# Gated attention with experts on one core: score products in two halves of 64 rows, value sums over 32 columns

## The chip, the core and the metric

The kernel runs on one core of a Trainium2 chip. The core has engines with a queue of their own each: TensorE (matmuls into PSUM; "PE", its weight loads "PEld"), VectorE ("DVE"), ScalarE ("ACT"), GpSimd ("POOL"), and SyncE ("SP"), which here issues all DMAs. They meet only through semaphores. The metric is device time in microseconds (us), lower is better.

## What is computed

Sixteen batches of 256 rows of width 128 pass through two layers. Each layer has a cross attention over 1601 context rows with 16 heads of 8 columns, a gated residual, then a second block with a gate: in layer 0 eight experts with two picked per row, in layer 1 a self attention plus eight experts. The second cross attention keeps only the 32 greatest scores of each row:

```
# layer 0 cross attention
scores = jnp.einsum('bhqd,bhkd->bhqk', q, k) / jnp.sqrt(jnp.float32(D_K))
attn = jax.nn.softmax(scores, axis=-1)
ctx = jnp.einsum('bhqk,bhkd->bhqd', attn, v)
# layer 1 cross attention
top_scores, top_idx = jax.lax.top_k(scores, 32)
w = jax.nn.softmax(top_scores, axis=-1)
out = jnp.einsum('bhqk,bhqkd->bhqd', w, top_v)
```

## The kernel before, in words

Heads are worked in groups of four (`HG`), four groups to a batch, 64 groups in all. A float32 score is computed as a bf16 product: q and k are split in three bf16 parts each, and six combinations of parts, of 8 columns each, are stacked as 48 rows (`ROWS`). Three further rows carry the row's shift (its maximum, or the least kept score), so that the attention's score product has 51 rows (`ROWX`) and comes out shifted. The tiles `q`, `k_scan`, `k_att` have 128 partitions, and the rows above 51 are filled with zeros once at the start by GpSimd, so every product contracts 128 rows.

For each group of layer 0, a scan finds the maximum of each row: `n0` (L611) multiplies 128 query rows with 512, 512, 512 and 65 keys, one product per step, into two PSUM banks `score` in turn; `n0_max` (L1056, VectorE) reduces each. `row_turn`, `row_minus`, `shift`, `rows_out`, `rows_in` then bring minus the maximum into the stack's three rows through DRAM. After that, for each of 13 chunks of 128 keys, `s_0` (L652) makes the four heads' scores, four products of 256 columns, in one of two `wide` PSUM tiles (two banks each), `exp_0` (L930, ScalarE) takes the exponential to `prob`, and `pv` (L698) sums values: four matmuls, one per head, with 9 weight columns (8 of v and a one that sums the weights), in four column strips of the array, written to four strips of the PSUM tile `att`.

For layer 1 the scan `c1` (L626) writes to `wide`, ScalarE copies the scores to SBUF (`c1_out`, L911), and VectorE ranks them (`rank`, MAX8 at L958 and on). Where a check finds that the quick ranking may have missed one, the whole row is ranked again (L1095 to L1110). The attention of layer 1 adds for each chunk a `cut` (L920, ScalarE) of what lies below the 32nd score, which `cut_add` (L674, TensorE) adds to the scores with a product by minus the identity before `exp_1`. The self attention has the same pieces on tiles `k_self`, `q_self`: `z_score` (L785) with `z_max` (L1072), `s_z` (L664), `pv_z`.

The order of work on each engine is a timetable written out by hand: every step has a tick and is sorted by tick, and within a tick by the list `ORDER`. A group takes 32 ticks; layer 0's and layer 1's groups of different batches run side by side, so that score products of all kinds, value sums, the experts' float32 products (L740, L753) and the small transposes alternate on TensorE. Each step waits on semaphores for what it needs, e.g. `n0` for the maximum two steps back:

```
if i >= 2:
    q.wait_ge(sem["score_max"], i - 1)
```

SyncE issues one DMA for a scan tile (`k_scan`, L1407), one for a block of attention keys (`k_att`, L1437), one for queries (L1394), in the same way.

## Time and profile before

| | us |
|---|---|
| Median of 3 runs (6196.12 to 6210.12) | 6209.23 |
| The profiled execution | 6214.0 |
| its span, first to last instruction | 6212.0 |
| TensorE busy (78%) | 4855.6 |
| VectorE busy (76%) | 4696.6 |
| ScalarE busy (65%) | 4011.8 |
| GpSimd busy (14%) | 867.1 |

A busy share is an average over stages with different bounds. Matmuls are pipelined: one row of the timeline that joins several gives the time from the first start to the last end, so the cost of one more in a row is the difference between two such rows. The granted clock is TensorE's, 1.00 at 2.4 GHz and 0.50 at 1.2 GHz.

### The profile page before, as it was taken

The numbers are of one execution on the slowest core, as the hardware profiler recorded it, in microseconds if no ns is written. First come the engines' busy times: TensorE is split into PE (matmuls) and PEld (weight loads), VectorE is DVE, ScalarE is ACT, GpSimd is POOL, SyncE is SP. The second block draws the span as 40 slices with busy tenths as digits, with TensorE's granted clock in tenths as the row PEclk, the third lists the DMA queues.
The fourth block names the chain that finished last, engine by engine and source line by source line (L and its number), as shares of the span: only waits on it lengthen the run. The fifth ranks groups of instructions, "written<-read, shape, count | busy, mean of one in ns | idle before, by whom it ended". The sixth has DMA issues, their size and how long they took to land. (4 is left out here: it accounts for less than half of the span.)

```text
span 6212.0 us, 109517 instructions
## 1 busy us (share of the span) xinstructions
PE 4855.6 (78%) x34758; PEld 2301.8 (37%) x34758; DVE 4696.6 (76%) x23731; ACT 4011.8 (65%) x5196; POOL 867.1 (14%) x1650
## 2 busy tenths in 40 slices
PE   4878678888777888688788878887788788878676
PEld 2424234343433434243343434334343343434222
DVE  3476987869788686877868687787878868686872
ACT  1447656767575676676667676775767567676663
POOL 4111111111111111111111111111111111010000
PEclk7879989999898999899899999998999899999887
DMA  4222212222122222222222222221222222121110
GB/s 106 65 68 52 59 42 53 67 48 63 43 62 48 52 63 55 60 47 54 60 49 61 50 64 53 55 65 42 63 50 63 51 46 63 33 60 25 31 29 17
DMA packets 356330, 332.18 MB, mean 53 GB/s; under 512 B 102074, under 2 KB 313149, under 8 KB 355711
## 3 DMA queue, kind: packets, MB, share of 16 engines
q1 hardware_dynamic: 355710, 324.84, 22.4%
q8 instruction: 277, 4.54, 0.3%
q14 instruction: 343, 2.80, 0.2%
HBM read 217.54 MB, written 107.13 MB: 52 GB/s over the span
## 5 line engine op out<-in xcount | busy, mean ns | idle before, releaser
L958 DVE MAX8 cand<-s 128x8 f32<-128x67 f32 (+1 forms) x12288 | 2107.7, 214 | 29.9 <-DVEq L1110 18.0
L930 ACT ACTIVATE prob<-wide 128x1024 f32<-128x1024 f32 (+1 forms) x1792 | 1771.5, 1027 | 432.6 <-PE wide L652 232.2
L1056 DVE TENSOR_REDUCE part<-score 128x1 f32<-128x512 f32 (+1 forms) x2048 | 1151.0, 565 | 837.3 <-PE score L611 651.1
L911 ACT ACTIVATE s<-wide 128x1024 f32<-128x1024 f32 (+1 forms) x1024 | 857.1, 844 | 729.0 <-PE wide L626 431.2
L652 PE MATMUL wide<-q,k_att 128*128 128x256 bf16 (+1 forms) x6656 | 995.0, 283 | 180.2 <-ACT prob L930 88.1
L698 PE MATMUL att<-prob,v 128*9 128x256 f32 (+1 forms) x14336 | 1073.2, 399 | 60.8 <-ACT u L941 32.6
L920 ACT ACTIVATE below<-wide 128x1024 bf16<-128x1024 f32 (+1 forms) x832 | 809.8, 1023 | 276.6 <-PE wide L652 272.4
L611 PE MATMUL score<-k_scan,q 128*128 128x512 bf16 (+1 forms) x2048 | 710.2, 354 | 321.6 <-DVE part L1056 300.8
L674 PE MATMUL wide<-below,minus_ident 128*128 128x512 bf16 (+1 forms) x1664 | 512.4, 391 | 416.5 <-ACT below L920 416.2
L652 PEld LDWEIGHTS wide<-q,k_att 128*128 128x128 bf16 (+1 forms) x6656 | 594.1, 102 | 625.0 <-ACT prob L930 222.6
L626 PE MATMUL wide<-k_scan,q 128*128 128x512 bf16 (+1 forms) x2048 | 562.5, 360 | 139.2 <-ACT prob L930 70.3
L698 PEld LDWEIGHTS att<-prob,v 128*9 128x9 f32 (+1 forms) x14336 | 271.6, 91 | 490.4 <-issue 226.0
L611 PEld LDWEIGHTS score<-k_scan,q 128*128 128x128 bf16 x2048 | 203.1, 100 | 618.1 <-issue 289.1
L1329 POOL CAST shift<-minus 8x128 bf16<-8x128 f32 x192 | 54.1, 282 | 2522.8 <-issue 2243.9
L674 PEld LDWEIGHTS wide<-below,minus_ident 128*128 128x128 bf16 (+1 forms) x1664 | 96.9, 99 | 736.8 <-ACT below L920 736.8
L626 PEld LDWEIGHTS wide<-k_scan,q 128*128 128x128 bf16 x2048 | 142.9, 101 | 552.5 <-ACT prob L930 215.5
L753 PE MATMUL small<-w,hid 128*128 128x128 f32 x2048 | 302.9, 292 | 0.0
L1313 POOL CAST split_b<-split_f 128x512 bf16<-128x512 f32 (+2 forms) x192 | 91.7, 478 | 1411.7 <-issue 1397.5
L753 PEld LDWEIGHTS small<-w,hid 128*128 128x128 f32 x2048 | 253.4, 195 | 31.4 <-issue 0.9
L740 PE MATMUL wide<-v_xnT,w 128*128 128x256 f32 x1024 | 252.0, 402 | 9.2 <-ACT prob L930 9.1
L1241 DVE SCALAR_TENSOR_TENSOR v_acc<-small,v_one,v_acc 128x128 f32<-128x128 f32 x224 | 68.3, 347 | 234.9 <-PE small L753 234.9
L891 ACT ACTIVATE hid<-wide,b 128x256 f32<-128x256 f32 x512 | 199.0, 478 | 52.4 <-PE wide L740 50.9
(165 smaller groups left out, 5660.0 us busy)
## 6 DMA issues: line engine op xcount, KB each, us to landing
k_scan<-k_stack SPq DMA_DIRECT2D x512, 150.1 KB, 3.2
k_stack<-split_b SPq DMA_DIRECT2D x576, 128.0 KB, 2.5
k_att<-k_stack SPq DMA_DIRECT2D x384, 192.0 KB, 3.4
ctxT<-in_ctx_dram SPq DMA_DIRECT2D x32, 800.5 KB, 5.5
q_stack<-split_b SPq DMA_DIRECT2D x192, 64.0 KB, 2.1
q<-q_stack SPq DMA_DIRECT2D x128, 96.0 KB
self_stack<-split_b SPq DMA_DIRECT2D x192, 64.0 KB, 2.1
k_self<-self_stack SPq DMA_DIRECT2D x64, 96.0 KB
```

The source lines that it names most:

```text
L611: tensor.matmul(score[i % 2][:, 0:wd], m.q[0][g % QBUF[0]][:, hh, qt * P:(qt + 1) * P], m.k_scan[0][(HG * g + hh) % 2][:, a0:a0 + wd], sta ...
L626: r = tensor.matmul(ps[:, n0:n1], m.q[1][g % QBUF[1]][:, hh, qt * P:(qt + 1) * P], m.k_scan[1][(HG * g + hh) % 2][:, a0 + n0:a0 + n1], sta ...
L652: r = tensor.matmul(ps[0:kc, j * S:(j + 1) * S], m.k_att[kn % 3][:, j, c0:c0 + kc], rows[:, j, :], start=(j % 2 == 0), stop=(l == 0), skip ...
L674: r = tensor.matmul(ps[0:kc, x:x + BANK], m.minus_ident[0:kc, 0:kc], m.below[n % 2][0:kc, x:x + BANK], start=False, stop=True, skip_group_ ...
L698: r = tensor.matmul(att[32 * j:32 * j + HD + 1, 0:S], v[0:kc, c, j0 * HG + j, :], m.prob[n % 3][0:kc, j * S:(j + 1) * S], start=(c == 0), ...
L740: r = tensor.matmul(ps[:, k * S:(k + 1) * S], m.w_1[:, e, k * P:(k + 1) * P], m.xnT["v"][:, :], start=True, stop=True)
L753: r = tensor.matmul(ps[:, t * D:(t + 1) * D], hid[:, k, t * P:(t + 1) * P], m.w_2[:, e, k, :], start=False, stop=(k == PT - 1))
L911: scalar.activation(m.s[tile % 4][:, a0:a0 + wd], ps[:, 0:wd], ACT.Copy).then_inc(sem["wide_done"], 1)
L920: scalar.activation(m.below[n % 2][0:kc, :], ps[0:kc, :], ACT.Relu, scale=-STEEP).then_inc(sem["cut_done"], 1)
L930: scalar.activation(pr[0:kc, :], ps[0:kc, :], ACT.Exp, scale=SCALE).then_inc(sem["wide_done"], 1)
L958: i = vector.max(cand[:, c, :], s[:, KCUT[c]:KCUT[c + 1]])
L1056: vector.tensor_reduce(m.part[:, QT * hh + qt, c:c + 1], score[i % 2][:, 0:wd], AX.X, ALU.max).then_inc(sem["score_max"], 1)
```

## The change

A score product now contracts 64 rows, and two such products work on the two halves of the array: the tiles hold a second stack from partition 64 on (`UP`), with zeros in rows 51 to 63 of each half. Each half has its own PSUM bank.

- Scan (`n0`, `c1`): the lower half of `k_scan` holds keys 0 to 511 and 1024 to 1535, the upper 512 to 1023 and 1536 to 1600, and `q` holds the same stack in both halves. A step is now a pair, 512 with 512 columns or 512 with 65, at every second tick, and `n0_max` reduces both banks behind one wait for both.
- Attention (`s_0`, `s_1`, `s_z`, `z_score`): heads 0 and 1 of the group lie in the lower half, 2 and 3 in the upper, and the products alternate between the halves. `k_att` and `k_self` are half as wide.
- Value sums: each weight load reads 32 columns from the head's first column on, so also those of the next heads; they go to the rest of the strip of `att`, which nobody uses. The value tiles have 32 more columns at the end, and `pv` waits for all four parts of v instead of for its own.
- DMAs: a scan tile comes in three, queries, keys, rows in two each.
- GpSimd's fills follow the new shapes, the scan tiles' first.

```diff
@@ -217,9 +220,9 @@
         put("sp", at - 10, "q_in", 0, g)
         for hh in range(HG):
             put("sp", at + 8 * hh - 8, "k_scan", 0, g, hh)
-            for n in range(8):
-                put("pe", at + 8 * hh + n, "n0", g, hh, n)
-                put("dve", at + 8 * hh + n + 1, "n0_max", g, hh, n)
+            for n in range(2 * QT):
+                put("pe", at + 8 * hh + 2 * n, "n0", g, hh, n)
+                put("dve", at + 8 * hh + 2 * n + 1, "n0_max", g, hh, n)
         put("dve", at + SLOT + 1, "n0_all", g)
         rows(0, g, at + SLOT + 2)
...
+        m.v_flat = [[sb(f"v{l}_{n}", [P, NC * WIDTH + 32]) for n in range(2)] for l in range(2)]
+        m.v2_flat = sb("v2", [P, QT * WIDTH + 32])
...
-        m.k_att = [sb(f"k_att{n}", [P, HG, KB * P], BF16) for n in range(3)]
-        m.kq_self = [(sb(f"k_self{n}", [P, HG, S], BF16), sb(f"q_self{n}", [P, HG, S], BF16)) for n in range(2)]
+        m.k_scan = [[sb(f"k_scan{l}_{n}", [P, 2, BANK], BF16) for n in range(2)] for l in range(2)]
+        m.k_att = [sb(f"k_att{n}", [P, HALF, KB * P], BF16) for n in range(3)]
+        m.kq_self = [(sb(f"k_self{n}", [P, HALF, S], BF16), sb(f"q_self{n}", [P, HALF, S], BF16)) for n in range(2)]
         m.s = [sb(f"s{n}", [P, NK]) for n in range(4)]
         m.cand = [sb(f"cand{n}", [P, KC, 8]) for n in range(2)]
         m.left = sb("left", [P, KC, 8])
...
@@ -599,33 +608,31 @@

                     elif name == "n0":
                         g, hh, n = key
-                        i = turn("score", name, *key)
+                        (qt, c), i, kn = divmod(n, 2), turn("score", name, *key), HG * g + hh
                         if n == 0:
-                            kn = HG * g + hh
...
-                            q.wait_ge(k_scan_in[0][kn % 2], 16 * (kn // 2 + 1))
-                            q.wait_ge(q_in[0][g % QBUF[0]], 32 * (g // QBUF[0]) + 16)
-                        if i >= 2:
-                            q.wait_ge(sem["score_max"], i - 1)
-                        qt, c = divmod(n, 4)
-                        a0, wd = c * BANK, min(BANK, NK - c * BANK)
-                        tensor.matmul(score[i % 2][:, 0:wd], m.q[0][g % QBUF[0]][:, hh, qt * P:(qt + 1) * P],
-                                      m.k_scan[0][(HG * g + hh) % 2][:, a0:a0 + wd],
-                                      start=True, stop=True).then_inc(sem["score_full"], 1)
+                            q.wait_ge(k_scan_in[0][kn % 2], 48 * (kn // 2 + 1))
+                            q.wait_ge(q_in[0][g % QBUF[0]], 64 * (g // QBUF[0]) + 32)
+                        for x in range(2):
+                            r0, wd = UP * x, min(BANK, NK - (2 * c + x) * BANK)
+                            if i:
+                                q.wait_ge(sem["score_max"], 2 * i - 1 + x)
+                            tensor.matmul(score[x][:, 0:wd], m.q[0][g % QBUF[0]][r0:r0 + UP, hh, qt * P:(qt + 1) * P],
+                                          m.k_scan[0][kn % 2][r0:r0 + UP, c, 0:wd], start=True, stop=True,
+                                          tile_position=(r0, 0)).then_inc(sem["score_full"], 1)

                     elif name == "c1":
                         g, n, c = key
-                        hh, qt = divmod(n, QT)
-                        ps = fill(name, *key)
+                        (hh, qt), ps = divmod(n, QT), fill(name, *key)
...
+                        kn = HG * g + hh
                         if qt == 0 and c == 0:
-                            kn = HG * g + hh
-                            q.wait_ge(k_scan_in[1][kn % 2], 16 * (kn // 2 + 1))
-                            q.wait_ge(q_in[1][g % QBUF[1]], 32 * (g // QBUF[1]) + 16)
-                        a0, wd = c * 2 * BANK, min(2 * BANK, NK - c * 2 * BANK)
-                        for x in range(0, wd, BANK):
-                            n0, n1 = x, min(x + BANK, wd)
-                            r = tensor.matmul(ps[:, n0:n1], m.q[1][g % QBUF[1]][:, hh, qt * P:(qt + 1) * P],
-                                              m.k_scan[1][(HG * g + hh) % 2][:, a0 + n0:a0 + n1], start=True, stop=True)
-                        r.then_inc(sem["wide_full"], 1)
+                            q.wait_ge(k_scan_in[1][kn % 2], 48 * (kn // 2 + 1))
+                            q.wait_ge(q_in[1][g % QBUF[1]], 64 * (g // QBUF[1]) + 32)
+                        for x in range(2):
+                            r0, wd = UP * x, min(BANK, NK - (2 * c + x) * BANK)
+                            tensor.matmul(ps[:, x * BANK:x * BANK + wd],
+                                          m.q[1][g % QBUF[1]][r0:r0 + UP, hh, qt * P:(qt + 1) * P],
+                                          m.k_scan[1][kn % 2][r0:r0 + UP, c, 0:wd], start=True, stop=True,
+                                          tile_position=(r0, 0)).then_inc(sem["wide_full"], 1)

                     elif name == "row_turn":
...
@@ -644,26 +651,33 @@
                         rows, landed = m.q[l][g % QBUF[l]], q_in[l][g % QBUF[l]]
                         ps = fill(name, *key)
                         if c % KB == 0:
-                            q.wait_ge(k_att_in[kn % 3], 16 * (kn // 3 + 1))
+                            q.wait_ge(k_att_in[kn % 3], 32 * (kn // 3 + 1))
                         if c == 0:
-                            q.wait_ge(landed, 32 * (g // QBUF[l] + 1))
+                            q.wait_ge(landed, 64 * (g // QBUF[l] + 1))
                         c0 = c % KB * P
-                        for j in range(HG):
-                            r = tensor.matmul(ps[0:kc, j * S:(j + 1) * S], m.k_att[kn % 3][:, j, c0:c0 + kc],
-                                              rows[:, j, :], start=(j % 2 == 0), stop=(l == 0),
-                                              skip_group_check=True)
-                        r.then_inc(sem["wide_full"], 1)
+                        for h in range(HALF):
+                            for x in range(2):
+                                j, r0 = HALF * x + h, UP * x
+                                r = tensor.matmul(ps[0:kc, j * S:(j + 1) * S], m.k_att[kn % 3][r0:r0 + UP, h, c0:c0 + kc],
+                                                  rows[r0:r0 + UP, j, :], start=(h == 0), stop=(l == 0),
+                                                  tile_position=(r0, 0), skip_group_check=True)
+                                if h == HALF - 1:
+                                    r.then_inc(sem["wide_full"], 1)

                     elif name == "s_z":
                         g, c = key
                         k_self, q_self = m.kq_self[g % 2]
...
@@ -681,13 +695,13 @@
                         if name == "pv":
                             l, g, c = key
                             b, j0 = divmod(g, G)
-                            kc, end, v = chunk(NK, c), c == NC - 1, m.v[l][b % 2]
-                            q.wait_ge(sem["wide_done"], after("w_v_out", l, b, c // 4))
+                            kc, end, v = chunk(NK, c), c == NC - 1, m.v_flat[l][b % 2]
+                            q.wait_ge(sem["wide_done"], after("w_v_out", l, b, 3))
                             q.wait_ge(sem["wide_done"], after("exp_%d" % l, g, c))
                         else:
                             l, (g, c) = 2, key
...
@@ -695,7 +709,8 @@
                             if x:
                                 q.wait_ge(sem["att_out"], x)
                         for j in range(HG):
-                            r = tensor.matmul(att[32 * j:32 * j + HD + 1, 0:S], v[0:kc, c, j0 * HG + j, :],
+                            v0 = c * WIDTH + (j0 * HG + j) * (HD + 1)
+                            r = tensor.matmul(att[32 * j:32 * j + 32, 0:S], v[0:kc, v0:v0 + 32],
                                               m.prob[n % 3][0:kc, j * S:(j + 1) * S], start=(c == 0), stop=end,
                                               tile_position=(0, 32 * j), skip_group_check=True)
...
@@ -1047,31 +1065,32 @@

                     elif name == "n0_max":
                         g, hh, n = key
-                        qt, c = divmod(n, 4)
-                        i = turn("score_out", name, *key)
-                        q.wait_ge(sem["score_full"], i + 1)
+                        (qt, c), i = divmod(n, 2), turn("score_out", name, *key)
+                        q.wait_ge(sem["score_full"], 2 * i + 2)
                         if g and hh == 0 and n == 0:
                             q.wait_ge(sem["n0_ready"], after("n0_all", g - 1))
-                        wd = min(BANK, NK - c * BANK)
-                        vector.tensor_reduce(m.part[:, QT * hh + qt, c:c + 1], score[i % 2][:, 0:wd], AX.X,
-                                             ALU.max).then_inc(sem["score_max"], 1)
+                        for x in range(2):
+                            wd = min(BANK, NK - (2 * c + x) * BANK)
+                            vector.tensor_reduce(m.part[:, QT * hh + qt, 2 * c + x:2 * c + x + 1], score[x][:, 0:wd], AX.X,
+                                                 ALU.max).then_inc(sem["score_max"], 1)

                     elif name == "n0_all":
...
-                gpsimd.memset(m.v2[:, :, :, :], 1.0).then_inc(filled, 1)
-                for blank in (*m.q[0], *m.q[1], *(x for _, x in m.kq_self)):
-                    gpsimd.memset(blank[:, :, :], 0.0).then_inc(filled, 1)
-                for blank in (*m.k_scan[0], *m.k_scan[1]):
-                    gpsimd.memset(blank[:, :], 0.0).then_inc(filled, 1)
-                for blank in (*m.k_att, *(x for x, _ in m.kq_self)):
-                    q.wait_ge(filled, m.zeroed - 1)
-                    gpsimd.memset(blank[64:P, :, :], 0.0)
-                    gpsimd.memset(blank[32:64, :, :], 0.0).then_inc(filled, 1)
-                    q.wait_ge(filled, m.zeroed)
-                    gpsimd.memset(blank[32:ROWX, :, :], 1.0).then_inc(filled, 1)
-                    m.zeroed += 2
-                q.wait_ge(filled, 26)
+                    gpsimd.memset(m.v_flat[1][n][:, :], 1.0).then_inc(filled, 1)
+                gpsimd.memset(m.v2_flat[:, :], 1.0).then_inc(filled, 1)
+                for k_scan in (*m.k_scan[0], *m.k_scan[1]):
+                    gpsimd.memset(k_scan[:, :, :], 0.0).then_inc(filled, 1)
+                for heads in (*m.q[0], *m.q[1], *(q_self for _, q_self in m.kq_self)):
+                    gpsimd.memset(heads[:, :, :], 0.0).then_inc(filled, 1)
+                for n, keys in enumerate((*m.k_att, *(k_self for k_self, _ in m.kq_self))):
+                    gpsimd.memset(keys[:, :, :], 0.0).then_inc(filled, 1)
+                    for up in range(2):
+                        q.wait_ge(filled, 17 + 3 * n + up)
+                        gpsimd.memset(keys[UP * up + 32:UP * up + ROWX, :, :], 1.0).then_inc(filled, 1)
+                    q.wait_ge(filled, 19 + 3 * n)
                 for j in range(E):
...
                             q.wait_ge(sem["wide_full"], after("c1", (kn - 2) // HG, (kn - 2) % HG * QT + 1, 1))
-                        sync.dma_start(m.k_scan[l][kn % 2][0:ROWS, :], d.k_stack[l][b, :, :, kn % H, :]
-                                       .rearrange("n j s -> (n j) s")).then_inc(k_scan_in[l][kn % 2], 16)
+                        k_scan, stack = m.k_scan[l][kn % 2], d.k_stack[l][b, :, :, kn % H, :].rearrange("n j s -> (n j) s")
+                        for c in range(2):
+                            a0 = 2 * c * BANK
+                            wd = min(BANK, NK - a0 - BANK)
+                            sync.dma_start(k_scan[UP:UP + ROWS, c, 0:wd],
+                                           stack[:, a0 + BANK:a0 + BANK + wd]).then_inc(k_scan_in[l][kn % 2], 16)
+                        sync.dma_start(k_scan[0:ROWS, :, :], stack[:, 0:3 * BANK].rearrange("p (c s) -> p c s", s=BANK)
+                                       [:, 0:3:2, :]).then_inc(k_scan_in[l][kn % 2], 16)

                     elif name == "rows_out":
                         l, g = key
```

The first place is TensorE between two chunk pairs of layer 1's attention, in the middle of the run. L652 are the chunk pair's score products, L674 the cut's, L611 and L626 the two scans', L785 the self attention's, L698 the value sums. Before:

```order
L652 MATMUL wide<-q_0,k_att 128x256 x8
L674 MATMUL wide<-below,minus_ident 128x512 x4
L611 MATMUL score<-k_scan_1,q_0 128x512
L785 MATMUL score<-k_self,q_self 128x256 x2
L611 MATMUL score<-k_scan_1,q_0 128x65
L785 MATMUL score<-k_self,q_self 128x256 x2
L698 MATMUL att<-prob,v_1 9x256 x8
L626 MATMUL wide<-k_scan_1,q_1 128x512 x2
L611 MATMUL score<-k_scan_1,q_0 128x512
L785 MATMUL score<-k_self,q_self 128x256 x2
L652 MATMUL wide<-q_0,k_att 128x256 x8
L674 MATMUL wide<-below,minus_ident 128x512 x4
```

And now, where L661, L688, L619, L632, L802 and L713 are the same in that order:

```order
L661 MATMUL wide<-q_0,k_att 128x256 x8
L688 MATMUL wide<-below,minus_ident 128x512 x4
L619 MATMUL score<-k_scan_1,q_0 128x512
L619 MATMUL score<-k_scan_1,q_0 128x65
L802 MATMUL score<-k_self,q_self 128x256 x4
L713 MATMUL att<-prob,v_1 32x256 x8
L632 MATMUL wide<-k_scan_1,q_1 128x512 x2
L619 MATMUL score<-k_scan_1,q_0 128x512 x2
L661 MATMUL wide<-q_0,k_att 128x256 x8
L688 MATMUL wide<-below,minus_ident 128x512 x4
```

The scan's products stand two by two, where one stood at each tick; all score products alternate between the halves of the array, and the cut's still take the whole array between them.

The second place is VectorE, right behind a repeated ranking. L1056 (now L1074) are the scan's maxima, the others the ranking, L1072 (now L1091) the self attention's maxima. Before:

```order
L1056 TENSOR_REDUCE part<-score 128x1
L958 MAX cand<-s 128x8 x2
L981 MAX top<-left 128x8
L958 MAX cand<-s 128x8 x2
L984 MATCH_REPLACE left<-top,left 128x192
L958 MAX cand<-s 128x8 x2
L986 TENSOR_REDUCE eighth<-cand 128x1
L1056 TENSOR_REDUCE part<-score 128x1
```

And now:

```order
L1074 TENSOR_REDUCE part<-score 128x1 x2
L976 MAX cand<-s 128x8 x2
L999 MAX top<-left 128x8
L976 MAX cand<-s 128x8 x2
L1002 MATCH_REPLACE left<-top,left 128x192
L976 MAX cand<-s 128x8 x2
L1004 TENSOR_REDUCE eighth<-cand 128x1
L1091 TENSOR_REDUCE mx<-score 128x2 x2
L976 MAX cand<-s 128x8 x2
```

The maxima come in pairs, behind one wait, and only every second tick has one.

## Rows read from the trace of the kernel before

**Rows 1.** Busy time of each engine on the page, its share of the span, instructions.
```profile
PE 4855.6 (78%) x34758; PEld 2301.8 (37%) x34758; DVE 4696.6 (76%) x23731; ACT 4011.8 (65%) x5196; POOL 867.1 (14%) x1650
```

**Rows 2.** The waits of the whole span: us in all, times, longest.
```profile
DVE part L1056 <- PE score L611: 651.1, 494, 16.4
ACT s L911 <- PE wide L626: 431.2, 378, 6.0
...
ACT below L920 <- PE wide L652: 272.4, 274, 7.7
...
ACT prob L930 <- PE wide L652: 232.2, 303, 11.7
```

**Rows 3.** Busy us of PE, PEld, DVE, ACT, POOL in a batch's four groups; clock, DMA.
```profile
2126.00:2206.00 80.00, 63.08 (x505) 25.67 (x505) 66.27 (x346) 57.48 (x72) 9.55 (x27) 0.96 0.28 64
2206.00:2275.00 69.00, 55.13 (x449) 21.97 (x448) 62.48 (x342) 54.91 (x67) 13.48 (x20) 1.00 0.32 77
2275.00:2356.00 81.00, 69.16 (x494) 31.89 (x494) 68.10 (x380) 56.10 (x74) 9.57 (x22) 0.94 0.27 60
2356.00:2478.00 122.00, 104.61 (x729) 60.41 (x728) 81.99 (x409) 81.98 (x117) 19.04 (x33) 1.00 0.17 42
```

**Rows 4.** Timeline of TensorE from 3000 us: start, length, instructions joined.
```profile
3000.04 0.61 PE L652 MATMUL wide<-q,k_att 128*128 128x256 bf16 x4 [0.46 <-ACT s L911]
...
3002.79 0.42 PE L626 MATMUL wide<-k_scan,q 128*128 128x512 bf16 x2 [0.31 <-ACT prob L930]
3003.05 0.60 PE L611 MATMUL score<-k_scan,q 128*128 128x512 bf16 x2
...
3004.62 1.04 PE L652 MATMUL wide<-q,k_att 128*128 128x256 bf16 x8
...
3009.34 0.38 PE L611 MATMUL score<-k_scan,q 128*128 128x512 bf16 x1
3009.65 1.05 PE L698 MATMUL att<-prob,v 128*9 128x256 f32 x16
```

**Rows 5.** Groups of instructions by line: busy us, mean ns of one, idle before.
```profile
L652 PE MATMUL wide<-q,k_att 128*128 128x256 bf16 (+1 forms) x6656 | 995.0, 283 | 180.2 <-ACT prob L930 88.1 <-DMA k_att<-k_stack 25.0 <-ACT hid L891 25.0
...
L611 PE MATMUL score<-k_scan,q 128*128 128x512 bf16 (+1 forms) x2048 | 710.2, 354 | 321.6 <-DVE part L1056 300.8 <-DMA k_scan<-k_stack 17.4
...
L698 PEld LDWEIGHTS att<-prob,v 128*9 128x9 f32 (+1 forms) x14336 | 271.6, 91 | 490.4 <-issue 226.0 <-ACT prob L930 93.2 <-ACT u L941 48.7
L753 PEld LDWEIGHTS small<-w,hid 128*128 128x128 f32 x2048 | 253.4, 195 | 31.4 <-issue 0.9
...
L785 PE MATMUL score<-k_self,q_self 48*128 48x256 bf16 x512 | 104.4, 289 | 24.4 <-DVE mx L1072 23.9 <-DVE part L1056 0.2
```

**Rows 6.** Timeline of VectorE in the first group of heads.
```profile
77.17 2.22 DVE L1056 TENSOR_REDUCE part<-score 128x1 f32<-128x512 f32 x4 [0.57 <-PE score L611]
```

**Rows 7.** Timeline of GpSimd at the start, then one row of TensorE.
```profile
14.95 5.56 POOL L1284 MEMSET k_scan<- 128x1601 bf16 x4
20.56 1.80 POOL L1287 MEMSET k_att<- 64x2048 bf16 x1
...
37.20 0.95 POOL L1287 MEMSET k_self<- 64x1024 bf16 x1
...
43.59 0.61 POOL L1313 CAST split_b<-split_f 128x512 bf16<-128x512 f32 x1
...
50.17 0.69 PE L554 MATMUL small<-ident,xn 128*128 128x128 f32 x2 [34.63 <-DVE xn L1044]
```

**Rows 8.** Waits of SyncE's queue, then one row of its timeline.
```profile
SPq L1407 <- PE score L611: 1658.8, 190, 31.1
...
2028.47 0.81 SPq L1407 DMA_DIRECT2D k_scan<-k_stack  x2
```

**Rows 9.** Busy time in the last 200 us, then the clock over the run.
```profile
6000.00:6200.00 200.00, 131.41 (x776) 48.91 (x772) 82.08 (x438) 97.49 (x122) 17.11 (x44) 0.76 0.10 20
...
core 0: 6212.0 us, clock 0.918
```

123 lines of the change are left out of this document (71 added, 52 removed).

## The prediction, made before the changed kernel ran

> **What bounds the kernel now.** I read the page first. No engine fills the span: TensorE is busy 78%, VectorE 76%, ScalarE 65% [rows 1], with the span at 6212.0 us and the profiled execution at 6214.0, 5 us above the median of 6209.23. So the question is who waits for whom. The waits [rows 2] name TensorE most often: VectorE stands 651 us before the maxima of the scan (L1056) waiting for its score product, and ScalarE stands 431, 272 and 232 us before its three drains, each ended by a score product (L626, L652). That is 1586 us, ended by the products that the change touches. TensorE for its part waits 301 us for VectorE's maxima before L611 [rows 5]. It is a ring of short waits, so a microsecond saved on TensorE doesn't always reach the end.
>
> How much does, the windows tell [rows 3]. One batch takes four groups of heads, here 80, 69, 81 and 122 us (352 in all). In the 69 us group VectorE is busy 62.5 us, 91%: it is the bound, 6.5 us are idle. In the 80 and 81 us groups it is busy 66 and 68 us and TensorE 63 and 69: a mixed bound. In the 122 us group, with the experts' products, TensorE is busy 105 us and VectorE only 82: TensorE bounds.
>
> **The score products.** Four products of 256 columns take 0.61 us and eight 1.04, so one more costs (1.04 - 0.61)/4 = 0.1075 us [rows 4]. Two of 512 columns take 0.60 and one 0.38, so one more costs 0.22; a 512 with the narrow 65 takes 0.42, so that one costs 0.04. If the two halves of 64 rows stream side by side, half of each set disappears. The before trace has no product in row halves, but it has four products side by side in column strips: 16 instructions of L698, 256 columns each, take 1.05 us together, 0.066 each, less than the 0.1075 of L652 [rows 4]. The counts (half of them from the page's groups, the split of L611 and L626 into 1536 wide and 512 narrow from the loop: three of 512 columns and one of 65 for each of 512 row tiles) are [rows 5] (6656/4 = 1664 chunks of L652, 64 x 2 = 128 of L664 by its loop, 1536 and 512 of L611, L626 the same by its loop, 512 of L785):
> - L652 and L664: 1792 chunks x 2 x 0.1075 = 385 us
> - L611: 512 pairs of 512 x 0.22 + 512 x 0.04 = 133 us, and L626 the same, 133 us
> - L785: 256 of its 512 products x 0.1075 = 28 us
>
> Together 679 us, 42.4 a batch. Bounds: 0 (the halves run one after the other) to 679. I take the whole, being nearest to the strips of L698, and keep 0 for a rival.
>
> Rule beside it, not used in the sum: the Trainium skill, "TensorE: Matmul & The Clock Gate", section "Measured speedup vs the span model", gives 3.07x for four row tiles at N=512, not 4x. At the same efficiency two halves would give about 1.5x: an estimated saving of 450 us instead of 679, 190 instead of 291 at the end and a time near 6090. No row here shows row halves side by side.
>
> **The switches of shape.** A 512-column product followed by L698 starts it 9.65 - 9.34 = 0.31 us later, against the 0.22 between two of one shape [rows 4]: a change between shapes of the array costs 0.09 us. Before, the scan's, the attention's and the cut's products all have one shape; now the score products have another than L674, so each chunk pair goes there and back (the order's rows stand with the change). Over the program the order has 3818 changes of shape before and 5259 now: 1441 more, 90 a batch, 8.1 us a batch. Some lie under waits: before L674 TensorE waits for ScalarE's cut anyway. Bounds 0 and 130 us over the run; I take all of it against the saving, so TensorE is left with 42.4 - 8.1 = 34.3 us a batch less, 8.6 a group.
>
> **What reaches the end.** In the 69 us group, with 6.5 us to be had at most, a quarter, 2.2. In the two mixed groups a little over half, 4.5 each. In the 122 us group 80%, 7.0. That is 18.2 a batch and 291 us over 16. The shares are my choice: each follows how much busier the one engine is than the other. Bounds: the 122 us group alone, 112 us; all of it, 549 us.
>
> **VectorE's maxima in pairs.** The work is the same; a pair waits once for both halves, and TensorE may refill the first bank while the second is reduced. While other VectorE work stands between pairs this costs nothing and takes out half the meetings of the two engines. Without such cover it costs: in the first group alone, where four maxima take 2.22 us behind a wait of 0.57 [rows 6], i.e. 1.39 us for two, a pair would take 1.2 us and then wait for most of a fresh product, 0.6 to 0.8. That is some 0.5 us x 16 pairs = 8 us lost.
>
> **The start.** The first split by GpSimd waits behind its fills until 43.6 us, and TensorE waits 34.6 us for what follows from it [rows 7]. The key tiles are half as wide now: nine fills of 1.8 us and six of 0.94 become half as long (8.1 + 2.8 us), and four of 1.39 (5.56/4) shrink by 577 of 1601 columns (2.0): 13 us earlier. With the 8 lost above the start brings 5.
>
> **Sums over values.** 32 columns instead of 9 in each weight load: 91 ns for 9 columns and 195 for 128 [rows 5] make about 20 ns more for one. Within a group the loads lie under the running strips, so only the first load of a batch of chunks shows, some 900 x 0.02 = 18 us of TensorE; the matmuls stream the same 256 columns. I count 7 at the end. Bounds 0 and 40.
>
> **Transfers.** A key tile of the scan comes in three transfers instead of one, the other loads in two: 1024 + 512 + 128 + 128 + 192 = 1984 more, each about 0.4 us of SyncE's queue (two take 0.81 [rows 8]), 12 us in a group. SyncE's queue waits 1659 us for the scan's products alone [rows 8], so they are hidden; TensorE waited 17.4 us in all for scan tiles [rows 5]. If that cover were gone each scan tile would be 0.8 us late, 512 x 0.8 = 410 us at worst. I take 0.
>
> **The clock.** The granted clock was 1.00 in the 69 us group and 0.94 to 1.00 in the others, but 0.76 in the last 200 us, where TensorE has less to do [rows 3, 9]; over the run the mean is 0.918 [rows 9], so it sits at 1.2 GHz for 16% of the time. With some 11% less for TensorE to do there will be more such stretches. I take 10% of the time more, 600 us; TensorE streams about 45% of it, which doubles, 270 us, and a quarter of that reaches the end, since those are the stretches in which TensorE isn't the bound: 67 us. Bounds 0 and 320 (below).
>
> Sum: 6214 - 291 - 5 + 7 + 67 = 5992 for a profiled execution, and 5 less for the median: 5987.
>
> **Rivals.**
> - More of it arrives (16%). VectorE's 651 us of waiting fall by half because it meets TensorE half as often, 325 us instead of the share counted above, and the clock holds: about 5850. For it: 494 separate waits [rows 2]. Against: VectorE at 91% in one group.
> - VectorE holds the ring (12%). Only the 122 us group gains, 112 us, and the clock takes 67 back: 6160. For it: VectorE 66 to 68 us busy in the 80 us groups.
> - The clock takes it all (12%), slower. TensorE, idle more often, falls to 1.2 GHz for half of the time: 34% more, 2040 us, x 0.45 x 0.35 (it is then the bound more often) = 321 us against 291 gained: about 6240. It decides from 47% of the time at the low level on. For it: the last 200 us. Beside it, the Trainium skill, same page, "The HAM clock gate": throttled is the default and activity releases it; [rows 9] agree. Zero rows in the halves don't bring the streamed columns back.
> - The halves don't overlap (6%), slower. Nothing is saved; the switches cost 8.1 us a batch of which half counts, 66 us, and 494 waits of VectorE get 0.22 longer for the second half, 109: about 6380. This is also the case in which the change doesn't do what it says.
>
> **Chances.** My forecast, a part of the saving arrives, 54%, with its own range 5900 to 6110. A measurement of this kernel can't tell less than 0.3% from no change, 19 us. Faster: 54 + 16 and most of the third case, 0.79. Slower: 12 + 6 less a little, 0.16; same 0.05. Range for 8 in 10: from 5840, taking in the first rival, to 6220.
>
> **What would show it.** Four products of L652's successor should take near 0.40 us instead of 0.61, started in pairs within hundredths; two of 512 columns 0.38 to 0.40 instead of 0.60. VectorE's wait for the scan's product should fall below 450 us, and ScalarE's three below 700 in sum. The 122 us group should shrink most, the 69 us group least. The first split should start near 30 us. The granted clock should have a mean near 0.87; under 0.77 the third rival is at work. If pairs start 0.22 us apart, the fourth is. If VectorE is over 90% in all four groups, the second. I would be wrong above all if the low clock falls on the groups in which TensorE bounds.

## The result, and the profile after

The changed kernel takes 6538.43 us (median of 4 runs, 6524.7 to 6546.8) against 6209.67 for the kernel before: ratio 1.0536, 95% interval 1.0514 to 1.0558. It is slower, and lies outside the range of the prediction. The profiled execution took 6524.7 us, its span is 6522.7.

The page first, the row of busy times (answers to [rows 1]), then the clock over the run (to the last row of [rows 9]):

```profile
PE 4921.5 (75%) x34505; PEld 2089.1 (32%) x34758; DVE 4674.4 (72%) x23731; ACT 4003.7 (61%) x5196; POOL 856.6 (13%) x1650
```
```profile
core 0: 6522.7 us, clock 0.791
```

TensorE should have lost 679 us of score products, and is busy 66 us more than before, although 253 of its products (all of the cut, L688) are missing from this trace. The second row shows what else moved: the granted clock fell from 0.918 to 0.791. There are two levels, 1.00 (2.4 GHz) and 0.50 (1.2 GHz), so the time at the low level is 2 x (1 - clock) x span: 1019 us before, 2726 us after.

TensorE's timeline from 3000 us (start, length, instructions joined; answers to [rows 4]) goes over from the low level to the high one between two of its rows (the granted clock is 0.50 from 3000 to 3011.3 us and 1.00 from there to 3020):

```profile
3001.64 0.60 PE L619 MATMUL score<-k_scan,q 64*128 64x512 bf16 x2
...
3008.39 0.61 PE L661 MATMUL wide<-q,k_att 64*128 64x256 bf16 x4
...
3009.36 1.93 PE L713 MATMUL att<-prob,v 128*32 128x256 f32 x16
...
3012.43 0.39 PE L632 MATMUL wide<-k_scan,q 64*128 64x512 bf16 x2
...
3013.90 0.39 PE L661 MATMUL wide<-q,k_att 64*128 64x256 bf16 x4
...
3014.73 0.38 PE L619 MATMUL score<-k_scan,q 64*128 64x512 bf16 x2
```

At the high level a pair of 512 columns takes 0.38 to 0.39 us, as one product of that size did before (0.38), and four of 256 take 0.39 instead of 0.61 [rows 4]. So the halves do stream side by side, wholly. At the low level the pair takes 0.60 to 0.61, as much as two whole products took before at the high level; and the sixteen of the value sums, which the change left alone but for their weights, take 1.93 instead of 1.05.

The same in sum, by line (busy us, mean ns of one, idle before; answers to [rows 5], and the last row is the experts' product, which the change doesn't touch):

```profile
L713 PE MATMUL att<-prob,v 128*32 128x256 f32 (+1 forms) x14336 | 1266.6, 460 | 55.2 <-ACT prob L948 30.6 <-ACT u L959 24.0
L661 PE MATMUL wide<-q,k_att 64*128 64x256 bf16 (+1 forms) x6656 | 699.0, 301 | 252.2 <-ACT prob L948 114.7 <-ACT s L929 60.0 <-ACT hid L909 33.2
L688 PE MATMUL wide<-below,minus_ident 128*128 128x512 bf16 (+1 forms) x1411 | 522.5, 449 | 522.3 <-ACT below L938 521.8 <-issue 0.3
L619 PE MATMUL score<-k_scan,q 64*128 64x512 bf16 (+1 forms) x2048 | 513.7, 395 | 325.6 <-DVE part L1074 272.8 <-DVE mx L1091 30.0 <-DMA k_scan<-k_stack 16.3
...
L768 PE MATMUL small<-w,hid 128*128 128x128 f32 x2048 | 395.3, 352 | 0.0
```

Before, the value sums and the experts' product stood at:

```profile
L698 PE MATMUL att<-prob,v 128*9 128x256 f32 (+1 forms) x14336 | 1073.2, 399 | 60.8 <-ACT u L941 32.6 <-ACT prob L930 26.1
...
L753 PE MATMUL small<-w,hid 128*128 128x128 f32 x2048 | 302.9, 292 | 0.0
```

The score products did become cheaper in spite of the clock: L661 699.0 us instead of 995.0, L619 513.7 instead of 710.2. What stood beside them became dearer: the value sums 1266.6 us instead of 1073.2, the experts' product 395.3 instead of 302.9.

The waits (us in all, times, longest; answers to [rows 2]):

```profile
DVE part L1074 <- PE score L619: 556.3, 303, 17.4
PE wide L688 <- ACT below L938: 521.8, 752, 1.8
...
ACT s L929 <- PE wide L632: 364.3, 334, 7.0
...
ACT below L938 <- PE wide L661: 328.9, 189, 7.6
...
ACT prob L948 <- PE wide L661: 206.8, 113, 10.0
```

The waits on score products fell from 1586 us to 1456. VectorE's wait before `v_acc`, which ends with an experts' product, is one that grew, from 234.9 us to 395.9.

Where it is lost, the windows of the same batch's four groups tell (busy us of PE, PEld, DVE, ACT, POOL; clock, DMA; answers to [rows 3]):

```profile
2197.00:2277.00 80.00, 61.21 (x496) 20.37 (x498) 66.91 (x352) 56.32 (x72) 8.88 (x24) 0.79 0.26 66
2277.00:2347.00 70.00, 51.49 (x449) 16.28 (x452) 61.87 (x338) 55.01 (x67) 13.52 (x20) 0.90 0.31 79
2347.00:2433.00 86.00, 70.68 (x492) 27.58 (x494) 67.84 (x379) 56.44 (x74) 9.58 (x22) 0.81 0.23 58
2433.00:2569.00 136.00, 112.22 (x727) 62.22 (x728) 81.40 (x408) 81.94 (x117) 19.78 (x34) 0.86 0.15 39
```

The first two groups take what they took (80 and 70 us for 80 and 69), one of them even at 0.79. The third takes 5 us more, and the fourth, in which TensorE bounds, 14 more: 136 us at a clock of 0.86 where it was 122 at 1.00. That is 20 us in a batch of 352. The other batches agree: cut at the reductions `mx<-part`, of which each group has one, and without the first batch, the fourth group took 120.5 us at a clock of 0.97 in the mean of 15 batches before, and 135.7 at 0.82 after. That is 228 of the 311 us that the span grew; the other three groups together account for some 60.

Last the start (timeline of GpSimd, answers to [rows 7]): the first split begins at 30.76 us instead of 43.59.

```profile
30.76 0.61 POOL L1329 CAST split_b<-split_f 128x512 bf16<-128x512 f32 x1
```

### The profile page after: what moved, and what is told of

The parts are those of the page before. It is cut to its first block and busy times, and to the rows that moved or that the text cites. A ratio compares the mean times of both kernels' runs of the same rounds, so it can differ in the third digit from the quotient of the medians.

```text
span 6522.7 us, 111248 instructions
## 1 busy us (share of the span) xinstructions
PE 4921.5 (75%) x34505; PEld 2089.1 (32%) x34758; DVE 4674.4 (72%) x23731; ACT 4003.7 (61%) x5196; POOL 856.6 (13%) x1650
## 5 line engine op out<-in xcount | busy, mean ns | idle before, releaser
L948 ACT ACTIVATE prob<-wide 128x1024 f32<-128x1024 f32 (+1 forms) x1792 | 1765.8, 1027 | 479.8 <-PE wide L661 206.8
L1074 DVE TENSOR_REDUCE part<-score 128x1 f32<-128x512 f32 (+1 forms) x2048 | 1072.9, 566 | 713.7 <-PE score L619 556.3
L713 PE MATMUL att<-prob,v 128*32 128x256 f32 (+1 forms) x14336 | 1266.6, 460 | 55.2 <-ACT prob L948 30.6
L929 ACT ACTIVATE s<-wide 128x1024 f32<-128x1024 f32 (+1 forms) x1024 | 856.0, 842 | 696.0 <-PE wide L632 364.3
L938 ACT ACTIVATE below<-wide 128x1024 bf16<-128x1024 f32 (+1 forms) x832 | 808.9, 1022 | 330.3 <-PE wide L661 328.9
L688 PE MATMUL wide<-below,minus_ident 128*128 128x512 bf16 (+1 forms) x1411 | 522.5, 449 | 522.3 <-ACT below L938 521.8
L661 PE MATMUL wide<-q,k_att 64*128 64x256 bf16 (+1 forms) x6656 | 699.0, 301 | 252.2 <-ACT prob L948 114.7
L619 PE MATMUL score<-k_scan,q 64*128 64x512 bf16 (+1 forms) x2048 | 513.7, 395 | 325.6 <-DVE part L1074 272.8
L632 PE MATMUL wide<-k_scan,q 64*128 64x512 bf16 (+1 forms) x2048 | 462.3, 393 | 145.2 <-ACT prob L948 75.1
L713 PEld LDWEIGHTS att<-prob,v 128*32 128x32 f32 (+1 forms) x14336 | 371.3, 122 | 541.8 <-issue 324.3
L661 PEld LDWEIGHTS wide<-q,k_att 64*128 64x128 bf16 (+1 forms) x6656 | 256.6, 101 | 708.6 <-ACT prob L948 270.9
L768 PE MATMUL small<-w,hid 128*128 128x128 f32 x2048 | 395.3, 352 | 0.0
L688 PEld LDWEIGHTS wide<-below,minus_ident 128*128 128x128 bf16 (+1 forms) x1664 | 100.2, 102 | 810.3 <-ACT below L938 810.3
L1260 DVE SCALAR_TENSOR_TENSOR v_acc<-small,v_one,v_acc 128x128 f32<-128x128 f32 x224 | 68.3, 346 | 395.9 <-PE small L768 395.9
L768 PEld LDWEIGHTS small<-w,hid 128*128 128x128 f32 x2048 | 334.3, 248 | 40.5 <-issue 20.8
L619 PEld LDWEIGHTS score<-k_scan,q 64*128 64x128 bf16 x2048 | 130.2, 99 | 601.3 <-issue 349.4
L632 PEld LDWEIGHTS wide<-k_scan,q 64*128 64x128 bf16 x2048 | 100.8, 95 | 661.8 <-issue 265.3
```

The costliest lines, as they stand in the source:

```text
L619: tensor.matmul(score[x][:, 0:wd], m.q[0][g % QBUF[0]][r0:r0 + UP, hh, qt * P:(qt + 1) * P], m.k_scan[0][kn % 2][r0:r0 + UP, c, 0:wd], sta ...
L632: tensor.matmul(ps[:, x * BANK:x * BANK + wd], m.q[1][g % QBUF[1]][r0:r0 + UP, hh, qt * P:(qt + 1) * P], m.k_scan[1][kn % 2][r0:r0 + UP, c ...
L661: r = tensor.matmul(ps[0:kc, j * S:(j + 1) * S], m.k_att[kn % 3][r0:r0 + UP, h, c0:c0 + kc], rows[r0:r0 + UP, j, :], start=(h == 0), stop= ...
L688: r = tensor.matmul(ps[0:kc, x:x + BANK], m.minus_ident[0:kc, 0:kc], m.below[n % 2][0:kc, x:x + BANK], start=False, stop=True, skip_group_ ...
L713: r = tensor.matmul(att[32 * j:32 * j + 32, 0:S], v[0:kc, v0:v0 + 32], m.prob[n % 3][0:kc, j * S:(j + 1) * S], start=(c == 0), stop=end, t ...
L768: r = tensor.matmul(ps[:, t * D:(t + 1) * D], hid[:, k, t * P:(t + 1) * P], m.w_2[:, e, k, :], start=False, stop=(k == PT - 1))
```

## The experiments

Theory (C in the expectations): the halves save what was forecast, but the granted clock falls with the work that TensorE is given, and that costs more. Rivals: the weight loads of 32 columns (W), the maxima two by two (P), and the halves by themselves (their switches of shape, S, and banks). Ratios are to the kernel before, with their 95% interval. The clock and the profile rows of a run are those of its profiled execution, which need not be the median one.

**a1_nine.** The change with the value sums back at 9 columns:

```diff
-                            r = tensor.matmul(att[32 * j:32 * j + 32, 0:S], v[0:kc, v0:v0 + 32],
+                            r = tensor.matmul(att[32 * j:32 * j + HD + 1, 0:S], v[0:kc, v0:v0 + HD + 1],
```

> The changed kernel with its value sums back at 9 weight columns a head. Theory C (the clock: the halved score products leave TensorE so little to stream that it sits at 1.2 GHz for 42% of the time, and this costs more than the halves save): time within 20 us of 6538, granted clock within 0.01 of 0.791. Rival W (the weight loads of 32 columns, 122 ns against 91, lengthen the sums, whose busy time rose from 1073 to 1267 us): 6480 or less.

Measured 6532.91 us, 1.0508 (1.0485 to 1.0532), clock 0.781: as theory C had it. The wide loads cost nothing that can be told, and with them rival W goes.

**b1_k64.** The kernel before, its score products over 64 rows, one after the other:

```diff
-                            r = tensor.matmul(ps[0:kc, j * S:(j + 1) * S], m.k_att[kn % 3][:, j, c0:c0 + kc],
-                                              rows[:, j, :], start=(j % 2 == 0), stop=(l == 0),
+                            r = tensor.matmul(ps[0:kc, j * S:(j + 1) * S], m.k_att[kn % 3][0:64, j, c0:c0 + kc],
+                                              rows[0:64, j, :], start=(j % 2 == 0), stop=(l == 0),
```

and so for both scans (L611, L626) and for L664 of the self attention. Its `z_score` (L785) contracted 48 rows already (48*128 in [rows 5]), so that not every product before has 128 rows.

> The kernel before with score products that contract rows 0 to 63 alone, one after the other, nothing else changed: the same columns are streamed in the same order, but over half the rows, and the changes of shape appear. Theory C in the form that the clock goes by streamed columns: clock 0.91, and only the switches cost, about 6275. Theory C in the form that the rows count as well: clock 0.80 or less and 6450 or more. Rival S: the switches alone, up to 130 us, 6340 at most with the clock at 0.91.

Measured 7377.49 us, 1.1891 (1.1846 to 1.1935):

```profile
core 0: 7380.9 us, clock 0.699
```
```profile
PE 6336.4 (86%) x34758; PEld 2666.3 (36%) x34758; DVE 4741.8 (64%) x23731; ACT 4067.0 (55%) x5196; POOL 866.5 (12%) x1650
```
```profile
3010.00:3015.00 5.00, 5.00 (x27) 1.48 (x26) 3.93 (x20) 2.00 (x3) 0.00 (x0) 0.50 0.04 5
```

This is the run that says most. The same products in the same order, the same columns streamed, half of the rows of the array in use, and the clock falls from 0.918 to 0.699. The rows that were left out held zeros and shift nothing in the result, so rows of zeros count for the clock. And it is not that TensorE had less to do: it is busy for 86% of the span instead of 78%, and from 3010 to 3015 us it is busy without a break at the low level. Theory C had this as one of its two forms, the one in which the rows count. What else is new here are the changes between products of 64 and of 128 rows; the expectation put at most 130 us on them.

The run also gives a price of the low clock: 4443 us at the low level, 3424 more than before, and 1169 us more span, so **0.34 us for each microsecond more at the low level**, or 0.30 if the 130 us for the changes of shape are taken off first. The repeated executions of one kernel give another estimate, with no edit between them: they differ in clock and in span together, and a straight line through each kernel's own executions rises by 0.31 us a microsecond over all kernels (0.20 to 0.52 by kernel, few executions each).

**a2_fill, a4_fill4, b6_fill.** Ahead of each cut product, in the time in which TensorE waits for ScalarE's `below`, two (four) products with a tile of zeros, of 128 rows and 256 columns, are added into the half of `att` that nobody uses:

```diff
+                def filler(count):
+                    if m.closed:
+                        q.wait_ge(sem["att_out"], m.closed)
+                    for _ in range(count):
+                        tensor.matmul(att[:, S:2 * S], m.minus_ident[:, :], m.idle[:, :], start=False, stop=True,
+                                      skip_group_check=True)
...
+                        filler(2)
                         q.wait_ge(sem["cut_done"], n + 1)
```

> The changed kernel with two products of 256 columns more before each cut product (L688), 128 rows, of a zero tile, added to the unused second half of the att bank: work that nobody needs, put where TensorE waits for ScalarE's cut. Theory C: the granted clock rises from 0.79 to 0.84 or more and the time falls by 60 to 150 us, to 6390 to 6480. Rival S (the changes of shape of the array, 1441 more) and rival W: the added work costs what it doesn't hide, 0 to 90 us, so 6538 or more.

> The changed kernel with four added products of 256 columns of a zero tile before each cut product instead of two. Theory C (the clock decides): the clock rises further, to 0.88, and the time falls from 6318 to 6200 to 6270. Rival: the wait for the cut is filled by two already, so that the other two (832 x 2 x 0.107 = 178 us) stand on the path: 6330 to 6450.

> The kernel before with the same added work (two products of 256 columns of a zero tile before each cut product). Theory C: the granted clock rises from 0.92 to 0.95 and the time falls by 20 to 80 us, to about 6160. Rivals S and W: no effect on what they name, so 6210 plus what isn't hidden, up to 6290.

Measured: the change with two added 6318.23 us, 1.0182 (1.0160 to 1.0204), clock 0.844; with four 6232.47, 1.0038 (1.0022 to 1.0053), clock 0.860; the kernel before with two 6178.15, 0.9947 (0.9928 to 0.9965), clock 0.924. Work that computes nothing takes 306 of the 329 us back. Two added gained more than theory C said (it had 6390 to 6480), four came out in its range at a lower clock than its 0.88. In the kernel before the time fell as forecast, but the clock hardly moved, 0.918 to 0.924 where 0.95 was expected. Of a4_fill4, by line:

```profile
L577 PE MATMUL att<-idle,minus_ident 128*128 128x256 bf16 x3328 | 538.7, 288 | 0.0
...
L700 PE MATMUL wide<-below,minus_ident 128*128 128x512 bf16 (+1 forms) x1354 | 457.0, 402 | 173.2 <-ACT below L951 153.6 <-issue 11.1
```

The added products are busy 539 us, and TensorE's idle time before the cut product fell from 522 to 173: for the greater part they lie in a wait. (310 of the 1664 cut products are missing from this trace, 253 from that of the change; in b6_fill, where none is, the idle time fell from 416.5 us before to 234.4 for 325 us of added products.) The Trainium skill ("TensorE: Matmul & The Clock Gate", "The HAM clock gate") has the throttled clock as the default, which activity releases. These runs agree: more activity, zeros though it was, 0.791 to 0.844 and 0.860. That busy time alone isn't this activity, b1_k64 shows (busy 86%, clock 0.699).

**a5_fill64.** The four added products over rows 0 to 63 alone.

```diff
-                        tensor.matmul(att[:, S:2 * S], m.minus_ident[:, :], m.idle[:, :], start=False, stop=True,
+                        tensor.matmul(att[:, S:2 * S], m.minus_ident[0:64, :], m.idle[0:64, :], start=False, stop=True,
```

> The changed kernel with four added products of 256 columns before each cut product, as in the run with four that took 6232 us, but contracting rows 0 to 63 alone: the same time on TensorE at the same places, over half the rows. Theory C with rows: the added work counts half as much for the clock, so clock about 0.84 and 6290 to 6400. Rival (the added work helps by its place or its duration, not by the clock): 6232 within 20 us. Rival Z (half the rows don't hold the clock at all): 6500 or more.

Measured 6436.55 us, 1.0387 (1.0362 to 1.0412), clock 0.831. The instructions and their columns are those of a4_fill4, but they give back 102 us instead of 306: a third, less than the half that theory C had (6290 to 6400), and neither rival's number. So the rows count here too, on products that nobody waits for. Both this run and b1_k64 are why a streamed column of 64 rows mustn't be taken for one of 128 where the clock is asked about.

**a8_strips, a10_fillstrips.** To two (four) added products come four zero strips, side by side, before each of layer 0's value sums:

```diff
+                            for _ in range(1):
+                                for j in range(HG):
+                                    tensor.matmul(att[32 * j:32 * j + 32, S:2 * S], m.idle[:, 0:32], m.idle[:, :], start=False,
+                                                  stop=True, tile_position=(0, 32 * j), skip_group_check=True)
```

> The changed kernel with two added products before each cut and besides, before each value sum of layer 0, four strips of 256 columns of the zero tile in the shape of the value sums (0.107 us, no change of shape). Theory C: the stretches without a cut gain clock too, mean 0.88, time 6200 to 6280. Rival: TensorE bounds in those stretches, 832 x 0.107 = 89 us are added and half of them arrive: 6350 or more.

> The changed kernel with both additions: four products of 256 columns before each cut product and one round of four strips before each value sum of layer 0. Theory C: clock 0.875, 6150 to 6210. Rival: TensorE is full by now, 6250 to 6320.

Measured 6256.89 us, 1.0087 (1.0053 to 1.0121), clock 0.861, and 6205.25, 0.9999 (0.9987 to 1.0010), clock 0.872. Both times lie in theory C's ranges. The strips give 61 us beside two added products and 27 beside four. More help of this kind only brings the change level with the kernel before.

**b7_atthalf, a9_scanhalf, b5_pairs: the change in parts.** b7 has only the attention products of layers 0 and 1 in halves; a9 has everything but these; b5 is the kernel before, whole products of 128 rows, with layer 0's scan and the self attention's scan, products and maxima, two by two at every second tick.

```diff
-                put("pe", at + 8 * hh + n, "n0", g, hh, n)
-                put("dve", at + 8 * hh + n + 1, "n0_max", g, hh, n)
+                put("pe", at + 8 * hh + n // 2 * 2, "n0", g, hh, n)
+                put("dve", at + 8 * hh + n // 2 * 2 + 1, "n0_max", g, hh, n)
...
```

> The kernel before with the attention products of layers 0 and 1 (L652) in halves, the scans, the self attention and the value sums as before. Theory C: the 358 us of streaming that go are about half of the change's 679, so about half of the loss: clock 0.85, time 6330 to 6450. Rival S (changes of shape): the score products of the attention stand between products of another shape, so nearly all switches of the change appear here and the clock is as before: 6250 to 6340. Rival P (the scan's maxima in pairs are what costs): no more than 6210.

> The changed kernel with the attention products of layers 0 and 1 as before (128 rows, one after the other); the scans, their maxima in pairs, the self attention and the value sums as changed. Theory C: 321 us less of streaming, clock 0.86, 6300 to 6420. Rival P (the pairs): all of the loss is here, 6500 or more with a clock above 0.85.

> The kernel before with the scan's products of layer 0 (L611) and their maxima two by two at every second tick, and the self attention's score products likewise; each still over all rows, one after the other, with a wait of its own. Theory C: nothing happens to the streamed work, 6210 within 40 us, clock 0.92. Rival P (meeting in pairs costs VectorE its overlap with TensorE): 6280 or more with the clock unchanged.

Measured: b7 6287.5 us, 1.0121 (1.0084 to 1.0157), clock 0.873; a9 6374.34, 1.0274 (1.0249 to 1.0298), clock 0.862; b5 6257.58, 1.0085 (1.0063 to 1.0107), clock 0.908. a9 is as theory C had it and excludes rival P (6500 or more). b7 is a miss: its time lies in the range of rival S (6250 to 6340), below that of theory C, yet its clock fell to 0.873, where rival S asked for an unchanged one. b5 misses both: 53 us over the kernel before, more than the 40 of theory C, less than rival P's 6280, and at a lower clock than either had. The clock doesn't follow the changes of shape either, which excludes rival S as the cause of the loss. Counted in the traces (sides of the used array taken as 32, 64 or 128) there are 4065 before, 5820 in b8_attfill4 below, which is faster than the kernel before, and only 3797 in b5_pairs, which is slower; in the change, with its 253 records missing, 5219.

In b5 VectorE's wait is much shorter, against 651.1 before [rows 2]:

```profile
DVE part L1056 <- PE score L611: 460.4, 267, 16.2
```

And yet it is slower. A wait that is met half as often and shrinks by 191 us gave nothing that shows at the end; by the sums below the 49 us lost are the clock's, so it was not on the path. Why the clock fell here, with the same products over the same rows, stays open.

**b8_attfill4.** b7 with the four added products.

> Attention products of layers 0 and 1 in halves alone, and four added products of 256 columns of the zero tile before each cut product. Theory C: the added work lifts the clock from 0.873 to 0.91 and the time from 6288 to 6080 to 6180, faster than the kernel before. Rival: the wait for the cut is filled, no gain beyond 6210.

Measured 6086.49 us, 0.9824 (0.9798 to 0.9849): 1.8% faster than the kernel before, and in theory C's range. The same batch's groups, as in [rows 3]:

```profile
2082.00:2156.00 74.00, 60.98 (x553) 23.70 (x552) 65.27 (x343) 56.24 (x71) 8.97 (x25) 1.00 0.30 72
...
2306.00:2430.00 124.00, 110.28 (x783) 61.79 (x782) 82.42 (x410) 82.51 (x117) 19.42 (x34) 0.97 0.19 44
```

In this batch the first group gains, 74 us instead of 80, and the fourth is held at 124 (122 before, 136 in the change). Over 15 batches the mean of the fourth group is 119.5 us at a clock of 0.96.

**b8_attfill6, b8_attfillstrips, b9_attc1fill4.** From b8_attfill4 on: six added products; the strips of a8_strips (its expectation says 128 columns, but the edit and the trace have 256); layer 1's scan in halves too, without pairs of maxima:

```diff
+                        for x in range(2):
+                            r0, wd = UP * x, min(BANK, NK - (2 * c + x) * BANK)
+                            tensor.matmul(ps[:, x * BANK:x * BANK + wd],
+                                          m.q[1][g % QBUF[1]][r0:r0 + UP, hh, qt * P:(qt + 1) * P],
+                                          m.k_scan[1][(HG * g + hh) % 2][r0:r0 + UP, c, 0:wd], start=True, stop=True,
+                                          tile_position=(r0, 0)).then_inc(sem["wide_full"], 1)
```

> The version with the attention products of layers 0 and 1 in halves, with six added products of zero ahead of each cut product in place of four. If the wait ahead of the cut product still has room and the clock still rises: 6040 to 6080 at a clock over 0.935. Rival, that the wait is full: 6110 or more, with TensorE's idle time ahead of the cut product under 100 us.

> The version with the attention products in halves and four added products, with four zero strips of 128 columns more ahead of the sums over values in layer 0. Theory that low clock is left to win in layer 0: 6030 to 6080. Rival, that the strips stand on the path, as they did beside two added products only in part: 6110 or more.

> The kernel before with the attention products of layers 0 and 1 and the score products of layer 1's scan in halves of 64 rows, its maxima one at a time as before, and four added products of zero ahead of each cut product. Theory that the halves cost only through the granted clock: the added work holds it near 0.90, and it ends at 6040 to 6110, near the version with the attention alone in halves (6086). Rival, that the scan's halves cost by themselves: 6150 or more at a clock over 0.90.

Measured: 6092.85 us, 0.9823 (0.9792 to 0.9853), clock 0.930; 6104.57, 0.9831 (0.9805 to 0.9856), clock 0.927; 6175.42 (6138.17 to 6192.56, 10 runs), 0.9949 (0.9931 to 0.9967), clock 0.903 in its fastest execution (6138.17 us) and between 0.89 and 0.902 in the others. The first two fall between the numbers of theory and rival, and add nothing: the clock no longer rises, and more of the same gains nothing. The third misses its theory (6040 to 6110) and has the time of its rival, though seven of its ten executions lack the clock that the rival asks for, 0.90 or more; see the sums below.

**The sums.** Take 0.34 us off the span for each microsecond at the low level, the price from b1_k64 alone (which by that ends at 5870, as before), and what is left is a span without any low clock:

| | span | clock | us at the low level | span - 0.34 x low |
|---|---|---|---|---|
| before | 6212.0 | 0.918 | 1019 | 5866 |
| b5_pairs | 6260.6 | 0.908 | 1152 | 5869 |
| b7_atthalf | 6290.4 | 0.873 | 1598 | 5747 |
| a9_scanhalf | 6372.6 | 0.862 | 1759 | 5775 |
| after | 6522.7 | 0.791 | 2726 | 5596 |
| a2_fill | 6287.3 | 0.844 | 1962 | 5620 |
| a4_fill4 | 6232.4 | 0.860 | 1745 | 5639 |
| b8_attfill4 | 6063.2 | 0.929 | 861 | 5770 |
| b9_attc1fill4 | 6136.4 | 0.903 | 1190 | 5732 |

The runs left out of the table end at 5578 (a1_nine), 5677 (a5_fill64), 5664 (a8_strips), 5671 (a10_fillstrips), 5850 (b6_fill), 5798 (b8_attfill6) and 5803 (b8_attfillstrips). b6_fill has 325 us of added products and ends 16 below the kernel before, so differences of that size say nothing here.

At this price the change is worth 5866 - 5596 = 270 us, and the clock takes 0.34 x (2726 - 1019) = 580. The difference, 310, is the measured 311 by how the column is made, and the split goes with the price: at 0.30 it is 201 and 512. What tests it are the other rows. b5_pairs lands on 5869 though the price wasn't fitted to it: its 49 us are nearly all clock (0.34 x 133 = 45). The attention's halves are worth 119, the rest of the change 91, together 210 of the 270, so the parts don't add up to the whole. The added products cost 24 and 43 of their own. a5_fill64 is 182 us of span behind a4_fill4, of which the clock accounts for 0.34 x 423 = 144. b9_attc1fill4 is 38 better than b8_attfill4 in the last column and 112 worse by its clock. That speaks for the clock as the reason why b9_attc1fill4 was slow, but it is an account, not an experiment: no run held the clock beside scans in halves, so what they would do then stays open.

## Why the prediction was wrong

- **The clock** is the step that failed. The prediction took 10% of the time more at the low level, 600 us, at a price of 0.45 x 0.25 = 0.11, together 67 us. The runs show 1707 us more at a price of 0.34, together 580. Both factors were too small, by 2.8 and by 3. The share was taken from the 11% less that TensorE has to do; b1_k64 shows that products over 64 rows alone, with nothing less to stream, already lower the clock to 0.699. How much of the change's fall comes from the rows and how much from the halved streaming no run tells apart. The price assumed that low stretches fall where TensorE isn't the bound; the group in which it bounds went from 1.00 to 0.86 and from 122 to 136 us. The prediction named this as what would make it wrong above all, and expected that group to shrink most; it grew most. Its upper bound of 320 us was also too low, so the range couldn't hold the result.
- **The rival in which the clock takes it all** had the right mechanism and the right direction, with a chance of 12%; its sign (a clock mean under 0.77) nearly showed: 0.791. It priced the low clock at 0.16 and came out at 6240. It decided from 47% of the time at the low level; measured were 42%, and the clock had decided already. The sentence that zero rows don't bring the streamed columns back went into no sum; that the rows count by themselves stood in neither the forecast nor a rival.
- **The halves overlap**: right, 0.39 and 0.38 us as forecast. The estimate beside it, from the 3.07x for four row tiles in the Trainium skill ("TensorE: Matmul & The Clock Gate", "Measured speedup vs the span model"), made two halves 1.5x as fast; here the trace doesn't agree, the second half costs at most a hundredth of a microsecond (0.38 to 0.39 for two after, 0.38 for one [rows 4]).
- **What reaches the end**, with the switches: forecast 291 - 7 + 5 = 289 us, the account above says 270 at its price and 201 at 0.30. It is not shown more closely, nor by groups: no run had this change at a full clock. The 1441 changes of shape more are not confirmed by a trace: the count above gives 1154 more, with records missing.
- **The maxima in pairs**: the first group's maxima took 24.4 us for 21.9, so 2.5 us lost, not 8. Beyond it, b5_pairs gives 3 us more by the account: nothing, as forecast, though it ran at a lower clock, which nobody forecast. That VectorE's wait would fall under 450 failed (556.3); in a4_fill4, with more clock, it is 439.3, and b5_pairs speaks against this wait having set the time.
- **The start**: 12.8 us earlier, forecast 13.
- **Weight loads**: mean 122 ns for 32 columns against 91 for 9 before and 96 for 9 in a1_nine, at about the clock of the change; at the end nothing (a1_nine), forecast 7.
- **Transfers**: hidden, as forecast. TensorE waited 16.3 us for scan tiles, 17.4 before.
- **The three waits of ScalarE** should have been under 700 us in sum: 364.3 + 328.9 + 206.8 = 900. At the low level the products that they wait for are as long as before: four of 256 columns take 0.61 us.
- **The other rivals**: against the first, b5_pairs, where the waits were halved in number and nothing was gained; against the second, VectorE's share of the groups, 84, 88, 79 and 60% (66.91 of 80 us and so on), where it asked for over 90; against the fourth, the timeline, in which a pair takes as long as one product.

## What to carry to other kernels

Before TensorE is given less to do, ask what the granted clock will make of it, and price it: 2 x (1 - clock) x span is the time at the low level, and one run with the products over half the rows tells cheaply about what a microsecond of it costs (here 0.30 to 0.34). A saving on TensorE is worth most in the stages where it bounds, and so is the clock: see whether those stages still run at 1.00. If they don't, put the freed time where TensorE waits anyway, with products of zeros over the full 128 rows, and take only those savings that the clock survives: here the attention's halves with four added products, 6086 us, 1.8% under the kernel before.

## What the runs showed of the hardware that was not expected

- Products over 64 rows instead of 128, in the same order and with the same columns, took the clock from 0.918 to 0.699 (b1_k64, 18.9% slower), with TensorE busy 86% of the time instead of 78%. Added products of zeros over 128 rows raised it from 0.791 to 0.860, over 64 rows only to 0.831.
- Zeros hold the clock too: the moving tile of the added products has nothing else, and so had the rows that b1_k64 left out. Whether data would hold it better no run shows.
- Two products in the two halves of the array take no longer than one: 0.38 to 0.39 us at the high level for 512 columns, 0.60 at the low one, where a single product of 64 rows took 0.60 in b1_k64.
- Of 329 us lost, added work alone took 306 back, and the kernel before, at 0.918 already, still gained 0.5% by it.
